# A Hyena, linear-attention and mixture-of-experts kernel: five ranked parts, rows fetched two pairs ahead, and attention's matmuls moved in the slot

## The chip, the core and the metric

The kernel runs on one core of one Trainium2 chip. The metric is the device time of one execution in microseconds. A program for one core is timed several times; a profile comes from one execution more, whose own time is given beside its span.

## What is computed

Two layers over a tensor of 2 x 2048 tokens of width 128. Each layer normalises its input, adds an attention-like branch and a mixture of experts, and keeps the residual. The second layer is where the change lies:

```
xn = _layernorm(x)
x = x + L1_attn(xn) + L1_ffn(xn)

# L1_attn: linear attention with 16 heads of 8, features elu(t) + 1
q, k = fm(x @ wq + bq), fm(x @ wk + bk);  v = x @ wv + bv
kv = einsum('bnhd,bnhe->bhde', k, v)
z = 1 / (einsum('bnhd,bhd->bnh', q, k.sum(axis=1)) + 1e-6)
out = einsum('bnhd,bhde,bnh->bnhe', q, kv, z) @ wo + bo

# L1_ffn: 8 experts, the 2 with the largest norm are used for a token
gate_hidden = einsum('nh,erh->ner', x, W_A)
scores = sqrt(sum(gate_hidden ** 2, -1));  topk_scores, topk_idx = top_k(scores, 2)
w = softmax(topk_scores)
g = einsum('ner,efr->nef', gate_hidden, W_B);  up = einsum('nh,efh->nef', x, W_up)
y = einsum('nef,ehf->neh', silu(g) * up, W_down)
out = sum over the 2 chosen experts of w * y
```

The first layer (a Hyena operator by Fourier transforms, and eight experts and a shared one computed densely) is not edited.

## The kernel before

The 4096 tokens are 32 tiles of 128 (`T`), in 8 chunks of 4 tiles (`NCH`, `TPC`). There is no scheduler: every engine has its own program, written out in one order, and semaphores join them. After the first layer's Fourier part each engine walks through a list of `SLOTS` = 90 slots.

- Slots 0 to 47 are the first layer's dense experts, six slots a chunk (`N0` = 6): TensorE does `gate0` and `up0_step`, ScalarE a silu, VectorE `product0` (L1585), GpSimd a weighting (L888), TensorE `down0_step`. Neither the gate nor the up product of the next slot goes on without the silu and the product of the one before. Between them stand the chunk's output, its normalisation, keys and values, and the second layer's router: a step "due" at offset `at` runs for chunk c in slot at + 6(c + 1).
- The router ranks tiles in parts. Before, there are 4 parts of 8 tiles (`BT`), ready with chunks 1, 3, 5 and 7. For each part VectorE runs `rank` (three steps), TensorE `counts`, VectorE `slots` (L1482 to L1495, which gives every row its place) and `weigh` (L1680 to L1683), and GpSimd `scatter` (L858) writes the tile's rows twice, once for each chosen expert, to `expert_rows` in DRAM: 64 indirect DMAs in all.
- `tables` (L1506 to L1558, four steps on VectorE) makes from the counts a list of blocks of 128 rows that all go to one expert. There are 4 lists. Blocks are worked in pairs: `NP` = 36 pairs, 71 blocks. With `LISTED` = 0, 8, 24, 40, 71 the lists begin with pairs 0, 4, 12 and 20, and may be used when all rows of 8, 16, 24 and 32 tiles have landed.
- Pair i belongs to slot i + `PAIR0`, 52 before. SyncE loads its rows (`load_rows`, L722 to L726, a ring of 5 buffers). In a slot TensorE does `turn_rows(i + 1)` (L2075), `gate_up(i)` (the L1762, L1763 and L1764 matmuls on `rows_hi`), `turn_products(i - 1)` (L2104), `down_rows(i - 2)` (L2119), and then one or two steps of attention (L2139 two steps of sums, L2145 a transpose, L2150 the output product). ScalarE does `rows_hi(i + 1)` (L1087), a copy for attention, `silu_pair(i)` (L1094), `turned(i - 1)` (L1101). VectorE does `rows_lo(i + 1)` (L1598), its attention step (L1647 to L1650, L1659), `product(i)` (L1606), `places_of(i)`, `result_rows(i - 2)` (L1628), and whatever the router still has to do for chunks 5 and 7. GpSimd sends rows and results (L873), at most 3 in a slot (`PER_SLOT`), behind the slot's `gate_up`.
- After slot 30 of the pairs the results of the first 16 tiles are read back and added; those of the last 16 after the last pair.

The waits that the text below comes back to are these, in the kernel before:

```
# SyncE, load_rows(i), where pair i opens a list
sp.wait_ge(table_in, stage_of(i) + 1)
sp.wait_ge(rows_out[stage_of(i)], 16 * 2 * BT)
# GpSimd, in a slot of the pairs
pool.wait_ge(gu_mm, min(slot - PAIR0 + 1, NP))
# TensorE, turn_rows(i)
pe.wait_ge(ld_rows[i % RING], rows_loaded(i))
```

## Time and profile before

| | |
|---|---|
| median of 3 runs | 652.54 us (646.1 to 655.0) |
| the profiled execution | 649.94 us, span 648.1 us |
| mean granted TensorE clock | 0.973 |
| TensorE busy | 567.0 us (87%) |
| VectorE busy | 447.0 us (69%) |
| ScalarE busy | 300.8 us (46%) |
| GpSimd busy | 298.2 us (46%) |

The span runs from the first to the last instruction of the program; the 1.8 us beyond it are around the program. Busy time is summed over the whole span, so it says nothing of which wait sets the pace in a stage: for that the stages have to be read apart. Matmuls overlap in the pipeline, so a busy TensorE is not one at its peak.

### The profile page before, as it was taken

To read this page: it belongs to the slowest core of one execution; us is meant where nothing else is said; L and a number is where in the kernel's file an instruction comes from. 1 tells how busy PE (TensorE), PEld (TensorE's weight loads), DVE (VectorE), ACT (ScalarE), POOL (GpSimd) and SP (SyncE) were. 2 spreads that over 40 slices of the span, in tenths; PEclk is the share of its full clock that TensorE was granted. 3 is DMA by queue.
4 is the path that set the end of the run, shared out by engine and by line. 5 is a ranking of instruction groups with operands and counts; after the bars stand their busy time and mean duration, and the time that the engine had idled before them with its cause. 6 is when DMAs were issued, how large, how long until landed. Compare 5 with 4: busy or idle time off the path is not lost.

```text
span 648.1 us, 10568 instructions
## 1 busy us (share of the span) xinstructions
PE 567.0 (87%) x3218; PEld 467.6 (72%) x3218; DVE 447.0 (69%) x1199; ACT 300.8 (46%) x558; POOL 298.2 (46%) x268
## 2 busy tenths in 40 slices
PE   5899999989899998999999999986877877888870
PEld 2879985667687677888888878765665666777660
DVE  6858998729721992344659989987787685656673
ACT  4460247655424441344577657855835433334230
POOL 5610030006561563265334458768344755666661
PEclk9999999999999998999999999997999799999995
DMA  7350031400023502133222232122211232322626
GB/s 215 128 243 17 2 129 33 97 9 2 21 110 110 172 0 65 59 93 94 75 67 79 70 100 79 39 99 68 56 55 59 59 89 71 82 73 67 208 74 223
DMA packets 48381, 54.94 MB, mean 85 GB/s; under 512 B 7029, under 2 KB 40374, under 8 KB 47271
## 3 DMA queue, kind: packets, MB, share of 16 engines
q1 hardware_dynamic: 43542, 42.99, 21.2%
q0 software_dynamic: 4320, 8.99, 4.1%
q10 hardware_dynamic: 466, 2.31, 1.6%
q8 instruction: 28, 0.46, 0.3%
q14 instruction: 25, 0.20, 0.1%
HBM read 36.22 MB, written 15.94 MB: 80 GB/s over the span
## 4 chain that ended last, share of the span: by engine, by line
PE 30%; DVE 12%; issue 9%; ACT 6%; POOL 4%; another core or an unknown queue 4%; DMA 2%; SPq 1%; POOLq 0%; ACTq 0%; DVEq 0%
PE banks L1762 4%; PE banks L1764 4%; PE banks L1763 4%; PE banks L1968 3%; PE banks L1882 2%; PE banks L2119 2%; PE banks L1874 2%; POOL arena L888 1%; PE banks L2104 1%; PE banks L1895 1%; PE banks L1896 1%; DVE arena L1606 1%; DMA arena<-result_rows 1%; PE banks L2075 1%
## 5 line engine op out<-in xcount | busy, mean ns | idle before, releaser
L873 POOL DMA_INDIRECT result_rows<-arena x71 | 69.3, 975 | 38.8 <-PE banks L1764 16.6
L858 POOL DMA_INDIRECT expert_rows<-arena x64 | 63.6, 994 | 40.6 <-issue 14.6
L822 POOL TENSOR_TENSOR arena<-arena 128x512 f32<-128x512 f32 x32 | 40.8, 1275 | 86.2 <-DVE arena L1431 86.2
L888 POOL TENSOR_TENSOR arena<-arena 128x512 f32<-128x512 f32 x32 | 42.4, 1325 | 68.2 <-DVE arena L1585 68.1
L1585 DVE TENSOR_TENSOR arena<-banks,arena 128x512 f32<-128x512 f32 x48 | 33.0, 688 | 42.5 <-PE banks L1764 33.5
L1968 PEld LDWEIGHTS banks<-arena 128*128 128x128 f32 x384 | 48.8, 191 | 6.9 <-POOL arena L888 3.0
L1968 PE MATMUL banks<-arena 128*128 128x128 f32 x384 | 51.6, 277 | 1.9 <-DVE arena L1585 1.1
L1874 PE MATMUL banks<-arena 128*128 128x512 f32 x96 | 50.5, 608 | 2.4 <-DVE arena L1431 1.1
L1882 PEld LDWEIGHTS banks<-arena 128*128 128x128 f32 x256 | 33.0, 191 | 19.0 <-POOL arena L822 14.4
L2119 PE MATMUL banks<-arena 128*128 x284 | 39.6, 284 | 7.4 <-DVE arena L1628 4.0
L1087 ACT ACTIVATE rows_hi<-banks 128x256 fp32r<-128x256 f32 (+1 forms) x36 | 13.6, 379 | 67.7 <-remote 33.6
L1149 ACT ACTIVATE arena<-banks 128x512 f32<-128x512 f32 x48 | 28.7, 599 | 35.0 <-PE banks L1764 28.6
L980 ACT ACTIVATE arena<-banks 128x512 f32<-128x512 f32 x48 | 28.7, 597 | 32.5 <-PE banks L1850 32.5
L2119 PEld LDWEIGHTS banks<-arena 128*128 128x128 f32 x284 | 35.8, 197 | 9.0 <-issue 9.0
L1429 DVE TENSOR_TENSOR arena<-banks,arena 128x512 f32<-128x512 f32 x32 | 22.1, 692 | 23.7 <-PE banks L1874 22.1
L1882 PE MATMUL banks<-arena 128*128 128x128 f32 x256 | 34.4, 277 | 4.0 <-POOL arena L822 4.0
L1762 PE MATMUL banks<-gate_up_weights_hi,rows_hi 128*128 x71 | 32.3, 454 | 6.0 <-DVE arena L1606 4.6
L1009 ACT ACTIVATE arena<-banks 128x512 f32<-128x512 f32 x32 | 19.1, 597 | 39.4 <-PE banks L1882 39.4
L1438 DVE TENSOR_TENSOR arena<-banks,arena 128x512 f32<-128x512 f32 x16 | 11.1, 692 | 36.2 <-PE banks L1896 36.2
L1762 PE MATMUL banks<-projection_hi,xnt_hi 128*128 128x384 f32 (+1 forms) x92 | 33.4, 363 | 2.6 <-DVE xnt_lo L1247 2.6
L1606 DVE TENSOR_TENSOR arena<-banks,arena 128x512 f32<-128x512 f32 (+1 forms) x36 | 24.4, 677 | 11.8 <-ACT arena L1094 10.0
L1763 PE MATMUL banks<-projection_lo,xnt_hi 128*128 128x384 f32 (+1 forms) x92 | 31.9, 347 | 0.0
(281 smaller groups left out, 1628.7 us busy)
## 6 DMA issues: line engine op xcount, KB each, us to landing
arena<-expert_weights SPq DMA_DIRECT2D x64, 128.0 KB, 3.4
arena<-expert_rows SPq DMA_DIRECT2D x71, 66.0 KB
arena<-in_x SPq DMA_DIRECT2D x8, 512.0 KB, 6.8
arena<-result_rows SPq DMA_DIRECT2D x8, 512.0 KB
arena<-in_dft_f SPq DMA_DIRECT2D x1, 2048.0 KB, 9.6
normed_hi<-xnt_hi SPq DMA_DIRECT2D x1, 2048.0 KB, 6.4
normed_lo<-xnt_lo SPq DMA_DIRECT2D x1, 2048.0 KB, 10.9
arena<-in_dft_i SPq DMA_DIRECT2D x1, 2048.0 KB, 7.7
```

Of the source, the lines that this page charges most:

```text
L822: nc.gpsimd.tensor_tensor(out=T1[:, q % 3, :], in0=T1[:, q % 3, :], in1=T2[:, q % 2, :], op=ALU.add).then_inc(y_in, 1)
L858: pool.indirect_dma_start(out=xrows, out_offset=bass.IndirectOffsetOnAxis(ap=SLOT[:, k, t:t + 1], axis=0), in_=XNF[:, t, :], in_offset=Non ...
L873: pool.indirect_dma_start(out=yrows, out_offset=bass.IndirectOffsetOnAxis(ap=DEST[:, i, n:n + 1], axis=0), in_=YB[:, i % YBUFS, n, :], in_ ...
L888: nc.gpsimd.tensor_tensor(out=AM0[slot % 2], in0=AM0[slot % 2], in1=WB0[:, m, :], op=ALU.mult).then_inc(weighted, 1)
L1585: nc.vector.tensor_tensor(out=AM0[n % 2], in0=PS[1], in1=SG0, op=ALU.mult).then_inc(mult_done, 1)
L1606: nc.vector.tensor_tensor(out=AM1[:, i % 2, 0:n], in0=pair_banks(i)[:, 0:n, F1W:2 * F1W], in1=SG1[:, i % 2, 0:n], op=ALU.mult).then_inc(mu ...
L1762: mm(o, lh, rh, start=start, stop=False, skip_group_check=True)
L1763: mm(o, lh, rl, start=False, stop=False, skip_group_check=True)
L1874: mm(PS[2 + J % 2], TURNF, ZT[:, J % 2, :], start=True, stop=True).then_inc(d_mm, 1)
L1882: ins = mm(PS[6 + q % 2][:, P * n:P * (n + 1)], T1[:, q % 3, P * n:P * (n + 1)], TURNI, start=True, stop=True)
L1968: ins = mm(PS[2][:, D * t:D * (t + 1)], AM0[n % 2][:, P * t:P * (t + 1)], DW0[:, m, :], start=False, stop=(m == N0 - 1), skip_group_check= ...
L2119: ins = mm(PS[6][:, P * s:P * (s + 1)], AMT[:, i % 2, 2 * s + f, :], DN_FLAT[:, at], start=(f == 0), stop=(f == 1), skip_group_check=True)
```

## The change

The router's 32 tiles are ranked in five parts of 8, 4, 4, 8 and 8 tiles, and the four lists are made after 12, 16, 24 and 32 tiles. `LISTED` becomes 0, 16, 24, 40, 71, so the lists begin with pairs 0, 8, 12 and 20. Of the 64 scatters 24 instead of 32 stand ahead of the pairs; from slot 51 on they come at most three a slot (in slots 51 to 53, 55 to 60 and 64 to 69), behind the slot's gate and up products. Pair 0 moves to slot 51, so every pair stands one slot earlier beside the router's steps, whose slots stay. Rows are turned two pairs ahead, with a third pair of buffers. TensorE does a slot's gate and up products first, then the rows, then attention's steps, which come one pair later. ScalarE does the silu first, VectorE the product first and the results last. From pair 13 on the down products take turns in two banks. SyncE loads the 1 MB of down weights after pair 0's rows and no longer ahead of them.

```diff
-NBT = T // BT
+NBT = 4
+RANKED = (2 * TPC, TPC, TPC, 2 * TPC, 2 * TPC)
+RANKED_AT = tuple(sum(RANKED[:n]) for n in range(len(RANKED) + 1))
+LISTED_TILES = (0, *RANKED_AT[2:])
...
-LISTED = (0, *(2 * ((2 * BT * P * (n + 1) - E1 * (P - 1)) // P // 2) for n in range(NBT - 1)), NB)
+LISTED = (0, *(2 * ((2 * P * n - E1 * (P - 1)) // P // 2) for n in LISTED_TILES[1:NBT]), NB)
...
-WEIGH_AT = (20, 18, 18, 15)
+WEIGH_AT = (20, 18, 18, 18, 15)
...
-PAIR0 = 52
+PAIR0 = 51
 SLOTS = PAIR0 + NP + 2
-SCATTER_FROM = (33, 43, 54, 64)
-ROWS_FROM = 55
 RESULT_LAG = 1
-SCATTERS = ((1, 3, 3, 1, 1, 2, 1, 1, 3), (1, 1, 1, 3, 3, 2, 2, 2, 1))
-COUNT_BANK = (3, 3, 5, 5)
-COUNT_AT = (16, 16, 17, 14)
-RANK_AT = ((13, 14, 15),) * 3 + ((12, 13, 13),)
-TABLE_AT = ((19, 20, 21, 21),) * 3 + ((16, 17, 18, 19),)
+EARLY_ROWS = dict(zip(range(33, 48), (1, 3, 3, 1, 1, 2, 1, 1, 3, 1, 1, 1, 1, 2, 2)))
+ROWS_KNOWN = {PAIR0: 16, 55: 24, 64: 32}
+DOWN_IN_TWO = 13
+COUNT_BANK = (3, 3, 3, 5, 5)
+COUNT_AT = (16, 16, 16, 17, 14)
+RANK_AT = ((13, 14, 15),) * 4 + ((12, 13, 13),)
+TABLE_AT = ((17, 18, 18, 19),) + ((19, 20, 21, 21),) * 2 + ((16, 17, 18, 19),)
...
-            sp.wait_ge(u_mm, N0 * NCH)
-            sp.dma_start(DN_FLAT, w_dn).then_inc(ld_dn, 16)
...
-                    sp.wait_ge(rows_out[stage_of(i)], 16 * 2 * BT)
+                    sp.wait_ge(rows_out[stage_of(i)], rows_sent(stage_of(i)))
...
+                if i == 0:
+                    sp.wait_ge(g_mm, N0 * NCH)
                 load_rows(i)
+                if i == 0:
+                    sp.wait_ge(u_mm, N0 * NCH)
+                    sp.dma_start(DN_FLAT, w_dn).then_inc(ld_dn, 16)
...
+                if 0 <= i < NP:
+                    product(i)
+                if 0 <= i + 2 < NP:
+                    rows_lo(i + 2)
...
                 if st < NCH:
                     gate0(slot)
-                if 0 <= i + 1 < NP:
-                    turn_rows(i + 1)
                 if 0 <= i < NP:
                     gate_up(i)
+                if 0 <= i + 2 < NP:
+                    turn_rows(i + 2)
+                for n, step in attention_steps(i - 1):
+                    attention_step(n, step)
...
                 if 2 <= i < NP + 2:
                     down_rows(i - 2)
-                for n, step in attention_steps(i):
-                    attention_step(n, step)
```

Lines of the kernel after: `turn_rows` L2098, `gate_up` L1785 to L1787, attention L2165, L2171 and L2176, `turn_products` L2128, `down_rows` L2145 on TensorE; `product0` L1606, `tables` L1527 to L1579, `weigh` L1702 to L1705 on VectorE.

TensorE before, around the transposes of pair 20's rows (slot 71, which is pair 19's):

```order
L2119 MATMUL banks<-arena 128x128
L2139 MATMUL banks<-arena 128x144 x2
L2075 MATMUL banks<-arena 128x128 x2
L1762 ISA
L1762 MATMUL banks<-gate_up_weights_hi,rows_hi 128x512
L1763 REGISTER_ALU
L1763 MATMUL banks<-gate_up_weights_lo,rows_hi 128x512
L1764 MATMUL banks<-gate_up_weights_hi,rows_lo 128x512
```

TensorE in the kernel after, around the same transposes, which now stand in slot 69, pair 18's:

```order
L1786 MATMUL banks<-gate_up_weights_lo,rows_hi 128x512
L1787 MATMUL banks<-gate_up_weights_hi,rows_lo 128x512
L2098 MATMUL banks<-arena 128x128 x2
L2176 MATMUL banks<-arena 128x128 x4
L2088 TENSOR_LOAD arena
L2088 ISA x2
L2088 TENSOR_LOAD arena
L2088 ISA x2
L2128 MATMUL banks<-arena 128x128 x4
L2145 ISA
L2145 MATMUL banks<-arena 128x128
```

The transposes of pair 20 stood ahead of pair 19's gate and up products, and now stand right behind pair 18's; attention's step moved from the end of a slot to the place behind them.

VectorE before, from `product0` of slot 34 to that of slot 36 (L1585), with sums of squares, key bias and `normed_lo` between them:

```order
L1585 TENSOR_TENSOR arena<-banks,arena 128x512
L1450 TENSOR_REDUCE arena<-arena 128x8
L1585 TENSOR_TENSOR arena<-banks,arena 128x512
L1450 TENSOR_REDUCE arena<-arena 128x8
L1568 TENSOR_TENSOR arena<-banks,arena 128x2x256
L1576 TENSOR_TENSOR normed_lo<-banks,normed_hi 128x512
L1585 TENSOR_TENSOR arena<-banks,arena 128x512
```

VectorE after, from `product0` of slot 35 (L1606) on; `product0` of slot 36 follows four rows further on:

```order
L1606 TENSOR_TENSOR arena<-banks,arena 128x512
L1469 TENSOR_REDUCE arena<-arena 128x8
L1533 TENSOR_TENSOR arena<-arena 128x8
L1527 TENSOR_SCALAR arena<-arena 128x8
L1529 TENSOR_SCALAR arena<-arena 128x8
L1530 TENSOR_SCALAR arena<-arena 128x8
L1538 COPY arena<-arena 128x8
L1543 TENSOR_TENSOR arena<-arena 128x16
L1547 TENSOR_TENSOR arena<-arena 128x16 x4
L1589 TENSOR_TENSOR arena<-banks,arena 128x2x256
L1597 TENSOR_TENSOR normed_lo<-banks,normed_hi 128x512
L1702 TENSOR_SCALAR arena<-arena 128x4
```

The first list's tables, which stood in slots 31 to 33, and the new part's `weigh` now stand between the products of slots 35 to 38.

## Rows read from the trace of the kernel before

**Rows 1.** Stretches: length, then busy us (count) of each engine, TensorE clock, DMA

```profile
core 0: us, PE busy (x) PEld busy (x) DVE busy (x) ACT busy (x) POOL busy (x), PEclk, DMA share, GB/s
447.07:510.77 63.70, 51.90 (x287) 40.80 (x285) 46.30 (x176) 37.99 (x69) 32.84 (x31) 0.93 0.20 55
510.77:562.54 51.77, 40.97 (x275) 34.57 (x274) 36.62 (x145) 17.73 (x36) 31.18 (x33) 1.00 0.28 78
562.54:623.54 61.00, 51.47 (x345) 43.27 (x343) 37.72 (x140) 20.65 (x44) 37.48 (x39) 1.00 0.35 109
```

**Rows 2.** Waits of TensorE, 447.07 to 623.54: total us, times, longest

```profile
PE banks L2145 <- DVE arena L1650: 5.1, 4, 1.7
PE banks L1762 <- DVE arena L1606: 4.6, 7, 1.2
PE banks L2104 <- issue: 4.0, 9, 1.4
PE banks L2119 <- DVE arena L1628: 4.0, 4, 1.4
PE banks L2145 <- issue: 3.5, 3, 1.7
PE banks L2139 <- issue: 2.2, 1, 2.2
```

**Rows 3.** Timeline of TensorE, from 567 us

```profile
567.17 0.66 PE L2145 MATMUL banks<-arena 128*128 128x128 f32 x4 [1.67 <-DVE arena L1650]
```

**Rows 4.** Stretches of slots 31 to 34, 35 and 36, 37

```profile
365.20:382.80 17.60, 16.97 (x104) 14.12 (x102) 16.53 (x54) 11.89 (x23) 7.94 (x7) 1.00 0.21 52
382.80:388.50 5.70, 5.55 (x37) 4.78 (x35) 4.00 (x7) 2.66 (x5) 4.61 (x6) 1.00 0.56 167
388.50:393.76 5.26, 5.26 (x35) 4.40 (x34) 5.12 (x15) 4.21 (x9) 4.75 (x5) 1.00 0.13 45
```

**Rows 5.** Stretches of VectorE: the first list's tables, summed

```profile
sum 9.07, DVE 8.27; mean DVE 2.76
```

**Rows 6.** Stretches of VectorE: slots, then weigh

```profile
459.95:462.03 2.08, 1.84 (x12) 1.00 0.14 33
462.03:462.85 0.82, 0.72 (x7) 1.00 0.24 59
```

**Rows 7.** Stretches of VectorE: the three steps of ranking 8 tiles, summed

```profile
sum 5.25, DVE 5.01; mean DVE 1.67
```

**Rows 8.** Timeline of GpSimd: the last scatters

```profile
535.51 0.96 POOL L858 DMA_INDIRECT expert_rows<-arena  x1 [1.27 <-PE banks L1764]
...
540.57 0.95 POOL L858 DMA_INDIRECT expert_rows<-arena  x1 [0.30 <-issue]
```

**Rows 9.** Timeline of TensorE: pair 17, and the rows of pair 20

```profile
539.58 0.40 PE L1764 MATMUL banks<-gate_up_weights_hi,rows_lo 128*128 x1
...
548.55 0.44 PE L2075 MATMUL banks<-arena 128*128 128x128 f32 x2 [0.47 <-DMA arena<-expert_rows]
```

**Rows 10.** Chain of waits, from the last scatter to pair 20: start, us

```profile
540.57 2.14 DMA expert_rows<-arena
...
543.27 0.84 SPq L725
...
544.85 0.69 SPq L726
...
546.78 1.55 DMA arena<-expert_rows
```

**Rows 11.** Timeline of TensorE at both clocks: pairs 11 and 12

```profile
504.49 0.79 PE L1762 MATMUL banks<-gate_up_weights_hi,rows_hi 128*128 x1 [0.95 <-DVE arena L1606]
...
506.78 0.63 PE L1764 MATMUL banks<-gate_up_weights_hi,rows_lo 128*128 x1
...
510.77 0.48 PE L1762 MATMUL banks<-gate_up_weights_hi,rows_hi 128*128 x1
```

**Rows 12.** Timeline of TensorE: the router at slot 51, and pair 0

```profile
445.35 0.80 PE L1762 MATMUL banks<-router_weights_hi,normed_hi 128*128 128x512 f32 x1 [4.31 <-ACT arena L1068]
...
447.07 0.78 PE L1762 MATMUL banks<-gate_up_weights_hi,rows_hi 128*128 x1
```

**Rows 13.** Timeline of GpSimd: scatters of slot 47

```profile
434.33 0.99 POOL L858 DMA_INDIRECT expert_rows<-arena  x1 [0.17 <-issue]
```

**Rows 14.** Timeline of SyncE: down weights, then the rows

```profile
432.12 0.34 SPq L703 DMA_DIRECT2D arena<-in_w_dn  x1
433.81 4.78 SPq L726 DMA_DIRECT2D arena<-expert_rows  x4
```

**Rows 15.** Timeline of VectorE: the last results come back

```profile
639.70 0.69 DVE L1638 TENSOR_TENSOR arena<-arena 128x512 f32<-128x512 f32 x1 [7.28 <-DMA arena<-result_rows]
```

More of the change, by code:

```diff
@@ L541, in due, with ranked_due, ranked, list_of @@
             return c - 1 if rest == 0 and 0 <= c - 1 < NCH else None
-        def odd_due(s, at):
+        def ranked_due(s, at):
             c = due(s, at)
-            return c // 2 if c is not None and c % 2 else None
+            last = [n // TPC - 1 for n in RANKED_AT[1:]]
+            return last.index(c) if c in last else None
+        def ranked(n):
+            return slice(RANKED_AT[n], RANKED_AT[n + 1])
+        def list_of(t):
+            return sum(t >= n for n in LISTED_TILES[1:])
+        def rows_sent(k):
+            return 16 * 2 * (LISTED_TILES[k + 1] - LISTED_TILES[k])
         def attention_steps(i):
@@ L599, in shares @@
         def shares():
-            rows, results, of_slot = 2 * BT * 2, 0, {}
-            for slot in range(ROWS_FROM, SLOTS):
-                known = 2 * BT * (3 if slot < SCATTER_FROM[3] else 4)
+            rows, results, of_slot = sum(EARLY_ROWS.values()), 0, {}
+            for slot in range(PAIR0, SLOTS):
+                known = 2 * max(n for at, n in ROWS_KNOWN.items() if slot >= at)
                 n = min(PER_SLOT, known - rows)
@@ L619, in results_of, with down_bank @@
             return rows
+        def down_bank(i):
+            return PS[5 if i >= DOWN_IN_TWO and i % 2 else 6]
         def pair_banks(i):
@@ L906, in _ @@
                 for bt, at in enumerate(ROOT_AT):
[L907 removed]
+                    if ranked_due(slot, at) == bt:
                         root_of_norms(bt)
[L909 to L913 removed]
+                scatter(EARLY_ROWS.get(slot, 0))
                 if slot in share:
@@ L1701, in _ @@
                     negated_mean(c)
-                c = due(slot, 6)
+                c = due(slot, 6 if slot <= N0 * NCH else 5)
                 if c is not None:
@@ L1731, in _ @@
                         norm_sum(TPC * c + t)
-                for bt in range(NBT):
+                for bt in range(len(RANKED)):
                     for part, at in enumerate(RANK_AT[bt]):
-                        if odd_due(slot, at) == bt:
+                        if ranked_due(slot, at) == bt:
                             rank(bt, part)
-                for bt in range(NBT):
-                    for part, at in enumerate(TABLE_AT[bt]):
-                        if odd_due(slot, at) == bt:
-                            tables(bt, part)
+                for k in range(NBT):
+                    for part, at in enumerate(TABLE_AT[k]):
+                        if ranked_due(slot, at) == k + 1:
+                            tables(k, part)
+                if 2 <= i < NP + 2:
+                    result_rows(i - 2)
                 if i >= BACK_AT:
```

131 lines of the change are left out of this document (63 added, 68 removed).

## The prediction, made before the changed kernel ran

> **What bounds the kernel now.** I read the page's slices first and then cut the span where the code changes its kind of work. The pairs reach from 447.07 to 623.54 us, 176.5 us for 35 pairs. In the three stretches TensorE has 51.90 + 40.97 + 51.47 = 144.3 us of work, so it stands idle for 32.1 us; every other engine is busy for less than TensorE in each of them [rows 1]. TensorE paces this part, but something holds it up in most pairs. The table of its waits tells what: it adds up to 31 us, and the six rows shown carry 23.4 of them [rows 2]. The reader should see two things there. Attention's matmuls (L2139 and L2145) wait 10.8 us, for a VectorE step that was given to the same slot; an example is the 1.67 us at 567.17 [rows 3]. And the gate and up products (L1762) wait 4.6 us for VectorE's product of the pair before. For the part ahead of the pairs I then compared TensorE with VectorE slot by slot: TensorE is busy 16.97 of 17.60 us in slots 31 to 34 and 5.55 of 5.70 in slots 35 and 36, so it sets the pace there, while VectorE has 4.00 of 5.70 us filled; in slot 37 VectorE is at 5.12 of 5.26 [rows 4].
>
> **Attention behind gate and up, rows two pairs ahead.** No instruction comes or goes; waits do. Attention's matmuls now consume what VectorE made a slot earlier, so their 5.1 + 3.5 + 2.2 = 10.8 us should go. The product now leads VectorE's slot and gate and up TensorE's, so of L1762's 4.6 us I take 4 back. L2104 waits 4.0 us on ScalarE's copy, which also comes earlier: 2.5. L2119 waits 4.0 us for a bank to be read by the result copy (L1628); that copy moves to the end of VectorE's slot, and the second bank helps from pair 13 on: 1.7 [rows 2]. Sum **-19 us**. The bounds: in the last stretch a pair takes 61.00 / 13 = 4.7 us for 4.0 of work [rows 1]; if every wait went but those of the first 12 pairs' odd ones, 26 of the 32.1 us would; if a chain through ScalarE and VectorE (silu, product, transposes, copy) keeps most periods, only attention's longest waits go, which I put at 8, the 5.1 us row and part of the 3.5 one.
>
> **Rows of pair 20.** This is the cost. The last scatters stay in slot 69 but pair 20's rows are now turned in slot 69 too, directly behind the gate and up products whose end also releases those scatters. Before, slot 69 was pair 17's and all of pair 18's slot lay between: gate and up of pair 17 ended at 539.58 + 0.40 = 539.98 and the transposes came at 548.55, after a wait of only 0.47 us [rows 9]. From the start of the last scatter (540.57) to the end of the rows' load (546.78 + 1.55 = 548.33) there are 7.76 us: 2.14 for the scatter to land, SyncE's steps, the load [rows 10]. Two of SyncE's steps are slow ones of 0.84 and 0.69; without them it would be 6.2. The scatter itself starts later than its release: GpSimd's four earlier DMAs kept it from 535.51 to 540.57 [rows 8], so after a release it comes 0.3 us later (the gap between two DMAs) to 1.5. TensorE therefore waits 0.3 + 6.2 = 6.5 to 1.5 + 7.8 = 9.3 us, and nothing can fill it, since all later work on TensorE, and `rows_hi` and `rows_lo` of pair 20 on ScalarE and VectorE, stand behind in order. I take **+7.8**, nearer to the row as measured.
>
> The Trainium skill, "DMA: Bandwidth & Descriptors", section "Anatomy of one DMA — SWDGE (gpsimd) path", gives such a DMA a fixed cost of about 2.0 us, most of it the write's receipt, so no smaller transfer would shorten it. By that rule, the trace agrees: 2.14 us [rows 10].
>
> **Clock after it.** Behind a stretch with little TensorE work before 504.49 the same 512-column matmul took 0.63 us instead of 0.40 [rows 9, 11], and pair 11 took 510.77 - 504.49 = 6.28 us, all busy, where the mean of its stretch is 51.90 / 12 = 4.33 [rows 1]. A wait of 8 us for pair 20 should do that once: **+2.0** (0 to 2.5).
>
> **Rows of pair 12.** The same, but one pair of slack: its last scatters stand in slot 60, `turn_rows(12)` in slot 61. Of 6.5 to 9.3 us one pair is covered, 4.1 us of work (40.97 / 10) or 5.3 us with its waits (63.70 / 12) [rows 1]: 2.4 to 4.0, taken **+3.1**.
>
> **Pair 0 a slot earlier.** Its rows wait for the 24th scatter, the last of which starts about 434.33 [rows 13], landed at 436.5 by the 2.14 us of [rows 10]. SyncE's loads issued at 433.81 before, behind the down weights (432.12) [rows 14]; now they issue after 437 and land near 440.5 to 441.5. Then `rows_hi`, `rows_lo` and the gate products of pair 0 come in slots where the router's matmul waits 4.31 us anyway, until 445.35, for ScalarE [rows 12]. Gate and up of pair 0 start at 446 to 447, not one slot before 447.07. I take **+1.0** for a slot's work that does not leave the path, between -3 (a slot really gained) and +5 (the loads come last, behind the 1 MB of weights moving beside them).
>
> **VectorE in slots 35 to 38.** The first list's tables, 8.27 us of work in 9.07 us [rows 5], leave slots 31 to 33 and now stand ahead of `product0` of slots 36 to 38, with the new part's `weigh`, 0.82 [rows 6]. That adds 9.9 us. Off it go 0.5 (slot 37 ranks four tiles and not eight; a step takes 5.25 / 3 = 1.75 us [rows 7], and narrower ones save little) and VectorE's idle time there, 1.70 + 0.14 = 1.84 [rows 4]: 7.5 us of overflow, since the next slot's up products need `product0`. Slots 31 to 34 give back at most 17.60 - 16.97 = 0.6 [rows 4], because TensorE was full, even though their VectorE work now is the new part's rank and `slots` (2.08 [rows 6]) instead of tables. So 6.9; between 3 (the steps share out well over four slots, TensorE one slot ahead) and 7.5 I take **+6.5**.
>
> **At nothing:** the other tables (their work stays ahead of pairs 12 and 20 by whole slots, though beside a pair one earlier), the third buffers (SBUF only), the extra bank. The end is untouched: after the last pair GpSimd's result DMAs go back to back and VectorE waits 7.28 us for them [rows 15].
>
> **The sum.** -19 + 7.8 + 2.0 + 3.1 + 1.0 + 6.5 = +1.4 on the profiled execution's 649.94: 651.3. That execution is 2.6 us below the median of three, whose runs spread over 9 us; I predict **652**. The ends of all terms give 649.9 - 26 + 6.5 + 0 + 2.4 - 3 + 3 = 633 and 649.9 - 8 + 9.3 + 2.5 + 4.0 + 5 + 7.5 = 670; they will not all fall the same way.
>
> **Rivals.** (a) **Faster: rows do not hold TensorE.** If the last scatters start promptly and SyncE's steps are short, or TensorE reaches slot 69 late because it is held elsewhere, the 7.8, 2.0 and 3.1 vanish: 651.3 - 12.9 = 638. For it: SyncE's slow steps are rare. Against: the order puts the transposes right behind the releasing product, and the one such chain that the trace shows took 7.76 us. (b) **Slower: the reorder returns only 8 us**, because the silu, product, transpose, copy chain sets a pair's time once attention's waits are gone. Price 11 us: 662. It decides if pairs 22 to 34 keep a mean period over 4.5 us, where it was 4.7; for it speaks that waits listed without a releaser ("issue") carry a third of the six rows' time [rows 2]; against it, that pairs with no attention wait run at their work. (c) **The clock falls three times**, after the waits at pair 0, 12 and 20, not once: 2 x 2.0 more, 655. Against it: from 510.77 on no stretch of the pairs shows a clock below 1.00, in spite of waits of up to 2.2 us [rows 1, 2].
>
> The Trainium skill, "TensorE: Matmul & The Clock Gate", section "HAM oscillation — how this bites in real kernels", says that a kernel which waits for DMAs between short bursts of matmuls starts each burst at the gated clock, paying each time. By that rule (c) would hold at pair 0 and 20 surely, at 12 perhaps. The trace shows it once among the pairs, before pair 11 [rows 11], and not at waits of 2 us.
>
> (d) **The change does not do what it says**: pair 0 starts no earlier. The forecast has that in it already.
>
> **Chances.** Forecast .46, (a) .22, (b) .20, (c) .07, anything else .05. The range that leaves out about 2 in 10 runs from **637 to 665**: below it lie (a) with a deep reorder gain, above it (b) with the dear ends of the DVE or start terms. About 2% is what a measurement of this kernel can tell from no change: 639.5 and 665.6. Faster than that needs (a) and a gain of 19 or more (.13), or the forecast with a reorder gain near its bound (.07): .20. Slower needs (b) and dear terms (.06) or other mishaps (.04): .10. Same: .70.
>
> **What will show it.** In the table of TensorE's waits, L2165 and L2171 (attention) should be nearly gone, and rows of L2098 on the DMA of `expert_rows` should stand near pairs 12 (2 to 4 us) and 20 (6.5 to 9.3). Behind pair 20's, a pair of about 6 us with matmuls of 0.43 us, and a clock below 1.00 in that stretch. Pairs 22 to 34 at 4.0 to 4.3 us in the mean. Slots 35 to 38 some 7 us longer, with VectorE filled. The first L1785 of pair 0 at about the old distance from slot 34, plus those 7 us. I am wrong if pair 20's wait is under 3 us, if pairs keep 4.5 us or more, or if slots 35 to 38 keep their length.

## The result, and the profile after

The changed kernel took 675.49 us (median of 4 runs, 672.25 to 677.07), the kernel before 650.37 us in the same runs: ratio 1.039, 95% interval 1.034 to 1.044. It is 25 us slower, outside the range and on the side that had a chance of one in ten. Each time in this document is the median of all runs of a kernel; the ratios leave out a run that is over 1.5% above its kernel's fastest. The profiled executions differ by 27.1 us of span (675.2 against 648.1).

Where these 27.1 us arise is read by cutting both spans at the same work. The rows give, of the kernel after, each stretch's length, then busy time (and count) of TensorE, weight loads, VectorE, ScalarE and GpSimd, then TensorE's granted clock, DMA share and GB/s: the start up to slot 31, slots 34 to 39, slot 47 to pair 0, the pairs, the end.

```profile
0.00:372.05 372.05, 351.02 (x1883) 289.09 (x1884) 245.67 (x526) 172.71 (x315) 131.78 (x108) 0.99 0.26 82
...
382.65:410.91 28.26, 22.00 (x120) 18.77 (x119) 24.57 (x72) 14.73 (x24) 17.08 (x17) 0.82 0.23 69
...
444.32:459.45 15.13, 7.67 (x27) 5.75 (x28) 8.28 (x22) 6.33 (x13) 3.22 (x3) 0.66 0.37 117
459.45:646.54 187.09, 149.07 (x901) 128.58 (x900) 122.26 (x460) 76.13 (x149) 107.59 (x108) 0.91 0.26 77
646.54:675.20 28.66, 6.93 (x44) 6.26 (x42) 13.56 (x36) 2.45 (x5) 8.13 (x9) 0.68 0.44 149
```

The kernel before, cut at the same places:

```profile
0.00:369.30 369.30, 348.46 (x1883) 287.24 (x1884) 245.60 (x526) 172.73 (x315) 131.72 (x108) 1.00 0.26 82
...
433.30:447.07 13.77, 7.13 (x34) 5.49 (x35) 11.19 (x27) 7.60 (x16) 11.11 (x11) 0.83 0.45 150
447.07:623.54 176.47, 144.33 (x900) 118.65 (x898) 120.65 (x461) 76.38 (x148) 101.50 (x102) 0.97 0.27 80
623.54:648.10 24.56, 5.52 (x37) 4.84 (x37) 11.85 (x31) 1.96 (x4) 7.28 (x8) 0.63 0.50 171
```

The unedited start is 2.75 us longer, with 2.56 us more of TensorE's busy time for the same 1883 matmuls: the clock, and no effect of the change (in a second pair of profiles below, e13 and e16, the changed kernel comes to slot 31's product 2.7 us earlier, not later). Slots 31 to 47 add 8.3, slot 47 to pair 0 1.4, the pairs 10.6, the end 4.1. In the pairs TensorE is busy 4.7 us longer for the same work at a mean clock of 0.91 (before 0.97), and idle for 38.0 us where it was idle for 32.1. The table of its waits there (total us, times, longest) says why the idle time did not fall:

```profile
PE banks L2098 <- DMA arena<-expert_rows: 14.9, 3, 8.1
PE banks L2145 <- DVE arena L1650: 7.0, 5, 2.5
PE banks L2171 <- DVE arena L1672: 4.7, 2, 2.7
PE banks L1785 <- DVE arena L1628: 4.1, 5, 1.4
```

Against [rows 2]: the three waits for rows are new, L2145 (the down products, which wait for VectorE's result copy) has grown, attention's L2171 still waits 4.7 us although its input is now asked of VectorE a slot earlier. Without the waits for rows 23.1 us of idle time are left, 8.5 less than the 31.6 of before, so other waits did shrink; how much of that is the order's, the experiments below tell. The three waits for rows in TensorE's timeline (start, us, and in brackets the idle time before it and what ended it), with GpSimd's last scatter among them:

```profile
513.84 0.69 PE L2098 MATMUL banks<-arena 128*128 128x128 f32 x2 [3.80 <-DMA arena<-expert_rows]
...
556.46 0.96 POOL L881 DMA_INDIRECT expert_rows<-arena  x1 [0.30 <-issue]
...
563.26 0.69 PE L2098 MATMUL banks<-arena 128*128 128x128 f32 x2 [8.07 <-DMA arena<-expert_rows]
...
633.71 0.69 PE L2098 MATMUL banks<-arena 128*128 128x128 f32 x2 [3.06 <-DMA arena<-expert_rows]
```

They are pairs 12, 20 and 34. The second is the sum's largest cost as it was worked out: scatter 1.27 us after `gate_up(18)` ended at 555.19, rows 6.8 us later. The third I had not seen: SyncE issues the four 512 KB loads of the first results ahead of pair 34's rows, and these are now wanted a slot earlier.

Attention's wait is the line to dwell on. All three engines around 577 us:

```profile
573.14 0.66 PE L2165 MATMUL banks<-arena 128*128 128x144 f32 x4
...
573.74 0.63 PE L2128 MATMUL banks<-arena 128*128 128x128 f32 x4
577.73 0.19 DVE L1669 TENSOR_SCALAR arena<-banks 128x32 f32<-128x32 f32 x1 [2.87 <-remote]
...
578.51 0.60 ACT L1120 ACTIVATE arena<-banks 128x512 f32<-128x512 f32 x1 [4.52 <-remote]
578.82 0.31 PEld L2171 LDWEIGHTS banks<-arena 128*128 128x128 f32 x3 [2.19 <-DVE arena L1672]
```

TensorE ended the sums (L2165) at 573.8 and the transposes (L2128) at 574.4. VectorE and ScalarE, idle and waiting for just these, began at 577.7 and 578.5. The updates of the semaphores that they waited for stand in the trace at 577.70 and 578.49: TensorE's semaphore updates reached them 3.9 and 4.1 us after the work. The example that the prediction took for a same-slot dependency, [rows 3], has the same thing behind it in the kernel before:

```profile
561.91 0.66 PE L2139 MATMUL banks<-arena 128*128 128x144 f32 x4
565.15 0.43 DVE L1598 TENSOR_TENSOR rows_lo<-banks,rows_hi 128x256 fp32r<-128x256 f32 x1 [2.85 <-ACT rows_hi L1087]
...
566.09 0.18 DVE L1647 TENSOR_SCALAR arena<-banks 128x32 f32<-128x32 f32 x1
```

The sums ended at 562.6 and their update stands at 564.66; VectorE began on them at 566.1, held at 565.15 by rows that ScalarE had got late: the update of the rows' transposes stands at 564.71, 1.9 us behind their end. Below, an update is called late when its record stands over 0.4 us behind the last end of a TensorE instruction that raises the same semaphore.

By this count none of VectorE's or ScalarE's updates in the pairs is late in any trace of the table below. It is easy to think otherwise, because a part of the update records is missing wherever TensorE's come late: the pairs have 218 of VectorE's in the first profile of the kernel before and 377 in e16, the same kernel. In the stretch below (pair 22's product, then pair 23's gate products, which wait for it) the next record of the product's semaphore stands at 570.88, yet TensorE went on 0.15 us after the product's end:

```profile
567.03 0.68 DVE L1606 TENSOR_TENSOR arena<-banks,arena 128x512 f32<-128x512 f32 x1
567.86 0.49 PE L1762 MATMUL banks<-gate_up_weights_hi,rows_hi 128*128 x1
```

Whoever takes the next record of a semaphore for that of an instruction counts such updates as late too; the "about half of the time" of the first expectation below comes of that.

### The profile page after: what moved, and what is told of

It is laid out like the page before. It is cut to its first block, busy times and chain, and to the rows that moved or that the text cites. A ratio compares the mean times of both kernels' runs of the same rounds, so it can differ in the third digit from the quotient of the medians.

```text
span 675.2 us, 10610 instructions
## 1 busy us (share of the span) xinstructions
PE 578.6 (86%) x3222; PEld 484.0 (72%) x3222; DVE 454.4 (67%) x1228; ACT 302.6 (45%) x561; POOL 298.4 (44%) x270
## 4 chain that ended last, share of the span: by engine, by line
PE 30%; DVE 14%; issue 10%; POOL 5%; ACT 3%; DMA 3%; another core or an unknown queue 2%; SPq 1%; POOLq 0%; DVEq 0%; ACTq 0%
PE banks L1785 4%; PE banks L1787 4%; PE banks L1786 4%; PE banks L1991 3%; PE banks L2145 3%; PE banks L1905 2%; POOL arena L911 2%; PE banks L1897 2%; DVE arena L1628 1%; PE banks L1918 1%; PE banks L1919 1%; PE banks L2128 1%; DVE arena L1606 1%; POOL expert_rows L881 1%
## 5 line engine op out<-in xcount | busy, mean ns | idle before, releaser
L1606 DVE TENSOR_TENSOR arena<-banks,arena 128x512 f32<-128x512 f32 x48 | 33.1, 690 | 42.2 <-PE banks L1787 33.5
L1991 PEld LDWEIGHTS banks<-arena 128*128 128x128 f32 x384 | 49.8, 194 | 5.8 <-POOL arena L911 1.7
L1113 ACT ACTIVATE arena<-banks 128x512 f32<-128x512 f32 (+1 forms) x36 | 21.3, 590 | 67.0 <-PE banks L1787 64.1
L2145 PE MATMUL banks<-arena 128*128 x284 | 42.9, 300 | 8.6 <-DVE arena L1650 7.0
L1905 PEld LDWEIGHTS banks<-arena 128*128 128x128 f32 x256 | 33.6, 194 | 19.0 <-POOL arena L845 14.4
L2145 PEld LDWEIGHTS banks<-arena 128*128 128x128 f32 x284 | 39.1, 214 | 10.2 <-issue 10.2
L1785 PE MATMUL banks<-gate_up_weights_hi,rows_hi 128*128 x71 | 32.9, 463 | 6.2 <-DVE arena L1628 4.1
L1457 DVE TENSOR_TENSOR arena<-banks,arena 128x512 f32<-128x512 f32 x16 | 11.1, 692 | 39.2 <-PE banks L1919 39.2
L1120 ACT ACTIVATE arena<-banks 128x512 f32<-128x512 f32 (+1 forms) x36 | 21.5, 596 | 35.2 <-remote 17.6
L1785 PE MATMUL banks<-projection_hi,xnt_hi 128*128 128x384 f32 (+1 forms) x92 | 33.1, 360 | 2.6 <-DVE xnt_lo L1266 2.6
## 6 DMA issues: line engine op xcount, KB each, us to landing
normed_lo<-xnt_lo SPq DMA_DIRECT2D x1, 2048.0 KB, 10.8
```

Source lines behind the costliest of these rows:

```text
L1606: nc.vector.tensor_tensor(out=AM0[n % 2], in0=PS[1], in1=SG0, op=ALU.mult).then_inc(mult_done, 1)
L1785: mm(o, lh, rh, start=start, stop=False, skip_group_check=True)
L1905: ins = mm(PS[6 + q % 2][:, P * n:P * (n + 1)], T1[:, q % 3, P * n:P * (n + 1)], TURNI, start=True, stop=True)
L1991: ins = mm(PS[2][:, D * t:D * (t + 1)], AM0[n % 2][:, P * t:P * (t + 1)], DW0[:, m, :], start=False, stop=(m == N0 - 1), skip_group_check= ...
L2145: ins = mm(down_bank(i)[:, P * s:P * (s + 1)], AMT[:, i % 2, 2 * s + f, :], DN_FLAT[:, at], start=(f == 0), stop=(f == 1), skip_group_chec ...
```

## The experiments

Eighteen runs in five groups (e1 to e4, e5 to e8, e9 to e12, e13 to e16, e17 and e18), each group on one chip; each ratio is to the kernel before, run beside it on the same chip. That kernel's median was 648.6, 653.4, 629.9, 629.6 and 652.8 us in the five. The third and the fourth group ran on the same chip, the other three on three more. Late updates of TensorE in the pairs, counted in the traces (in brackets the time that at least one stood open):

```
                               pairs, us   late updates
before, first profile            176.5      63 (53.0 us)
changed, first profile           187.1      57 (45.0 us)
order alone (e1)                 179.6      76 (56.1 us)
before, direct results (e4)      155.0      16 (14.5 us)
order, direct results (e5)       165.9      15 (12.4 us)
changed, direct results (e6)     171.7      24 (19.3 us)
before, 4th group (e16)          158.7       0
order alone, 4th (e14)           162.6       0
changed, 4th (e13)               171.5       0
before, direct, 4th (e15)        155.6       0
before, two banks, 5th (e17)     176.3      61 (52.3 us)
```

**The order alone, twice (e1 and e14).** The changed kernel with

```diff
-RANKED = (2 * TPC, TPC, TPC, 2 * TPC, 2 * TPC)
-LISTED_TILES = (0, *RANKED_AT[2:])
-PAIR0 = 51
+RANKED = (2 * TPC,) * 4
+LISTED_TILES = RANKED_AT
+PAIR0 = 52
```

and the tables of slots and banks, and the waits that go with them, of the kernel before.

> The changed slot order alone (rows two pairs ahead, third buffers, attention behind gate and up, product and silu first, down products in two banks), with the four parts, the four lists and slot 52 of the kernel before. Theory of the prediction: the waits of TensorE in the pairs were same-slot dependencies, so the order returns 19 us (8 to 26): ratio 0.96 to 0.99, and no wait of attention's matmuls stays. Rival: these waits were semaphore updates that arrive 1 to 5 us after the work has ended, in stretches where GpSimd sends indirect DMAs (such updates stand open for about half of the time in both traces); they then move to other lines, and the order returns under 8 us: ratio 0.99 to 1.01.

Measured: 652.05 us, ratio 1.006 (1.000 to 1.012). It returned nothing. Its pairs:

```profile
445.37:624.92 179.55, 144.89 (x895) 124.50 (x893) 120.57 (x457) 76.02 (x148) 102.48 (x105) 0.94 0.27 79
```

TensorE's idle time there is 34.7 us (32.1 before), 5.8 of it waits for the rows of pairs 20 and 34.

> The slot order alone once more (1.006 in the first experiment). Without late updates it should show which waits it removes and which it adds: if attention's same-slot waits are real, the ratio is now below 0.99; if they were only late updates, it is 1.00 to 1.01.

Measured in the fourth group: 636.38 us, ratio 1.011 (1.007 to 1.016), so nothing without late updates either. Its pairs, and TensorE's waits in them:

```profile
446.35:608.94 162.59, 140.18 (x895) 122.74 (x893) 120.38 (x460) 76.58 (x148) 104.03 (x105) 0.95 0.30 88
```

```profile
PE banks L2147 <- DVE arena L1652: 11.0, 7, 2.4
PE banks L2100 <- DMA arena<-expert_rows: 4.9, 2, 2.7
PE banks L1787 <- DVE arena L1630: 1.9, 2, 1.0
```

L2147 is the down product: the order brings its own waits. The idle time is 22.4 us, where the kernel before has 17.8 in the same group (e16, below). The 4.9 us of L2100, the rows of pairs 20 and 34, are as much as the difference; the other waits changed their lines and kept their sum.

**The lists alone (e2).** The changed kernel with TensorE's, ScalarE's and VectorE's rows in a slot as before, rows one pair ahead, one bank.

> The five parts, the lists of 12 to 32 tiles and slot 51 alone, with the slot order of before (rows one pair ahead, one bank for the down products). Slots 34 to 39 should be as long as in the changed kernel (28 us for 17.5) with the clock at its lower level in part of them: about +11, and pair 0 about +1.4 more. Rows of pair 20 are turned at the head of the next slot, in effect the same place, so a wait of 6 to 8 us stays and the clock falls after it: +8. If lists and order simply add up to the changed kernel's 25 us, this one is at 1.03 to 1.05 and the order alone near 1.00; if the order was worth 19 us but was eaten by its waits for rows, this one is below 1.03.

Measured: 666.23 us, 1.027 (1.021 to 1.032), a little under the range. The wait for pair 20's rows was 3.9 us, not 6 to 8: here TensorE's transposes, down products and attention of the slot stand between the releasing product and the rows. The parts about add up: 2.7% for the lists and 0.6 to 1.1% for the order, 3.9% together.

**Pair 0 back in slot 52 (e3), and scatters released a slot earlier (e8).**

```diff
-PAIR0 = 51
+PAIR0 = 52
```

> The changed kernel with pair 0 back in slot 52 and nothing else: every list has one slot more between its last scatter and the transposes of its first rows. If the waits of 8.1 us (pair 20) and 3.8 us (pair 12) come from the scatters' place, they fall to about 4 and 0, the clock stays up at pair 20, and the kernel gains 8 to 10 us on the changed one (ratio to before 1.02 to 1.03). If TensorE would wait for something else there anyway, it is within 3 us of the changed kernel.

Measured: 664.60 us, 1.021 (1.014 to 1.028). The wait at pair 20 fell from 8.07 to 4.11 us, and that at pair 12 went. The clock did not stay up at pair 20 as expected: it stood at 0.50 from 552.0 to 558.9 us.

```diff
+                    if slot > PAIR0:
+                        pool.wait_ge(gu_mm, min(slot - PAIR0, NP))
+                    scatter(share[slot][0])
                     pool.wait_ge(gu_mm, min(slot - PAIR0 + 1, NP))
-                    scatter(share[slot][0])
```

> The changed kernel, but in the pairs' slots GpSimd's scatters of rows wait for the gate and up products of the slot before, and only the result DMAs for those of the slot itself. If the waits for rows come from where the scatters are released, the 8.1 us at pair 20 fall to about 4 and the 3.8 us at pair 12 to about 0, some 8 us in all with the clock (ratio near 1.025, as with slot 52). If GpSimd's own backlog holds the scatters (five DMAs of 1.26 us stand before the last), the wait falls by 2 us at most.

Measured: 679.97 us, 1.039 (1.031 to 1.048). The wait at pair 20 fell to 4.7 us and that at pair 12 went, yet the time did not: TensorE's idle time in the pairs was 40.6 us (38.0), now on L2173, L2147 and L2130. GpSimd's earlier DMAs are the likely cause, which was not tried apart.

**Results by direct DMAs (e4, e15, e5, e6).** The results' rows then lie elsewhere, and the sums at the end add other rows.

```diff
-                    pool.indirect_dma_start(
-                        out=yrows, out_offset=bass.IndirectOffsetOnAxis(ap=DEST[:, i, n:n + 1], axis=0),
-                        in_=YB[:, i % YBUFS, n, :], in_offset=None).then_inc(st_rows[i % YBUFS], 16)
+                    at = 2 * i + n
+                    at = YFIRST + P * at if at < 2 * T else P * (at - 2 * T)
+                    pool.dma_start(yrows[at:at + P, :],
+                                   YB[:, i % YBUFS, n, :]).then_inc(st_rows[i % YBUFS], 16)
```

> The kernel before, but GpSimd sends each block of results by a direct DMA of the same bytes to consecutive rows, not by an indirect one; so the results' rows lie elsewhere and the sums at the end add other rows. If the indirect form is what delays the semaphore updates, the late ones vanish in the pairs and with them most of TensorE's 32 us of waits there: ratio 0.96 or less. If the delay comes from GpSimd's queue as such or from something else, the ratio stays 0.99 to 1.01 and late updates stay as many.

Measured: 628.50 us, 0.970 (0.965 to 0.975). Late updates fell from 63 to 16, all of them before 533 us, where the scatters of rows, still indirect, run too. Length, busy time and clock of its pairs:

```profile
450.84:605.79 154.95, 139.81 (x899) 118.00 (x898) 120.67 (x461) 77.72 (x148) 75.58 (x104) 0.98 0.31 92
```

From pair 18 on no pair of this kernel has a wait over 0.4 us before pair 35, with attention's matmuls where the kernel before has them. The direct DMAs also write to consecutive rows and not to scattered ones; which of the two matters was not tried apart.

> The kernel before with direct result DMAs once more (0.970 in the fourth experiment; other rows are added at the end). If late updates are what direct DMAs save, it saves nothing on a chip without them: ratio 0.995 to 1.005. If an indirect DMA costs by itself, it is 0.97 on any chip.

Measured: 625.31 us, 0.992 (0.988 to 0.995). Where no update is late, direct DMAs are worth 5 us and not 20.

> The slot order alone (as in the first experiment) with the results sent by direct DMAs to consecutive rows, so the output adds other rows at the end. The kernel before with direct results took 0.970 of before, and TensorE still stood idle for 15 us in its pairs. If the order removes real same-slot waits and was only masked by late semaphore updates, it now returns part of these 15: 5 to 10 us below that one, ratio 0.955 to 0.962. If the order has nothing to give even then, the ratio is 0.970 again, within 0.005.

Measured: 637.81 us, 0.972 (0.966 to 0.979). No gain on the 0.970 of the order of before.

> The changed kernel with the results sent by direct DMAs to consecutive rows (other rows are added at the end). If late updates cost the changed kernel as much as the kernel before, it gains 20 us: ratio about 1.01. Slots 34 to 39 and the waits for rows stay, so it should not come below 1.00. If it gains more than 25 us, indirect result DMAs also lengthened the waits for rows.

Measured: 653.54 us, 0.9985 (0.994 to 1.003): 0.04 less than the changed kernel, some 26 us. That is over the 25 us of the expectation, yet the waits for rows hardly moved (13.4 us in its pairs, 14.9 in the changed kernel); where the rest comes from is open. Against e4 the ratio is 1.029, over two groups.

**The change and the kernel before without late updates (e13, e16).** Both unedited.

> The changed kernel once more, unedited, beside the kernel before on one chip. In the last four runs the kernel before took 630 us and not 649 to 653, and next to no semaphore update came late, with all indirect DMAs in place. If this chip is like that one, the changed kernel shows what it costs without late updates: the order 0 to 3, the waits for rows 12, VectorE's slots 8, the clock in the rest, ratio 1.03 to 1.04. If late updates made up much of its loss, the ratio falls to 1.01 to 1.02. If this chip has late updates, the ratio is 1.034 to 1.044 again.

Measured: 654.09 us, 1.040 (1.034 to 1.045). The change costs the same with and without late updates, within the intervals.

> The kernel before, unedited, for a profile on this chip. On a chip without late updates TensorE's waits on attention's matmuls (10.8 us in the first profile) should be gone, its idle time in the pairs about 15 us, and the span near 628 us; on one with late updates it is as in the first profile.

Measured: 630.87 us, span 629.0. The pairs of e16 and, below, of e13:

```profile
446.06:604.80 158.74, 140.98 (x899) 118.13 (x898) 121.69 (x464) 78.45 (x149) 104.36 (x104) 0.98 0.31 89
```

```profile
456.50:628.02 171.52, 142.01 (x902) 123.91 (x900) 122.89 (x463) 77.32 (x150) 107.94 (x108) 0.94 0.28 84
```

TensorE's waits in them, e16 first:

```profile
PE banks L1762 <- DVE arena L1606: 4.8, 8, 1.3
PE banks L2119 <- DVE arena L1628: 2.7, 1, 2.7
PE banks L2139 <- DVE arena L1650: 2.1, 2, 1.4
PE banks L2145 <- DVE arena L1650: 1.6, 1, 1.6
```

```profile
PE banks L2098 <- DMA arena<-expert_rows: 11.4, 3, 7.4
PE banks L1785 <- DVE arena L1628: 6.7, 4, 2.7
PE banks L2145 <- DVE arena L1650: 5.9, 4, 2.5
```

Attention's 10.8 us are 3.7 here, in the same kernel. The same step of pair 22 that waited 1.67 us at 567.17 in [rows 3] starts at once:

```profile
553.73 0.66 PE L2139 MATMUL banks<-arena 128*128 128x144 f32 x4
...
556.00 0.18 DVE L1647 TENSOR_SCALAR arena<-banks 128x32 f32<-128x32 f32 x1
...
557.16 0.60 PE L2145 MATMUL banks<-arena 128*128 128x128 f32 x4
```

**Filler for the clock (e7, e11).** Ahead of the transposes of three pairs, and in the second kernel ahead of the router's matmul in slot 51:

```diff
-                pe.wait_ge(ld_rows[i % RING], rows_loaded(i))
...
+                for _ in range({0: 7, 12: 3, 20: 9}.get(i, 0)):
+                    split_product(PS[0], (GUH_FLAT[:, 0:P], GUL_FLAT[:, 0:P]), (GUH_FLAT[:, 0:4 * P], GUL_FLAT[:, 0:4 * P]))
+                pe.wait_ge(ld_rows[i % RING], rows_loaded(i))
```

> The changed kernel with filler matmuls (128 x 512, their products are overwritten) ahead of the transposes of pairs 0, 12 and 20: 21, 9 and 27 of them, a little less than the waits there at the 0.23 us that one takes at the upper clock. The waits for rows themselves stay. If the lower clock after these waits is a cost of its own, the work behind them runs at 2.4 GHz (granted clock 1.00 around pairs 0, 12 and 20) and the kernel gains 3 to 6 us on the changed one (ratio 1.03); if idle time was what counted and the clock beside it nothing, the kernel is within 2 us of the changed one or slower.

Measured: 670.49 us, 1.023 (1.015 to 1.032), where the changed kernel has 1.039. The two were not run on the same chip. The ratios put the gain at 10 us, the two profiled spans at 3.7, and the ends of the intervals at 1 to 19: there is a gain, and its size is not settled. The clock did not stay up: it no longer fell ahead of pair 0, but stood at 0.50 for 3.4 us each from 513.4 and 554.4 us (6.8 and 10.3 us in the changed kernel). The pair with the wait for pair 20's rows took 12.19 us in place of 14.32, at a clock of 0.91:

```profile
555.66:567.85 12.19, 11.37 (x58) 9.32 (x57) 2.77 (x9) 1.58 (x3) 2.87 (x3) 0.91 0.18 51
```

> The kernel before with 15 filler matmuls (128 x 512, 3.5 us at 0.23 each, their products are overwritten) ahead of the router's matmul in slot 51, where TensorE waits 4.3 us for ScalarE and the clock falls for 7 us. If the clock is a cost of its own there, pair 0 starts at the upper clock and 1 to 3 us are won (ratio 0.995 to 0.998); if TensorE's filler delays something, or the pairs are held by other engines, no gain.

Measured: 631.77 us, 1.002 (0.998 to 1.006). This one decides nothing: on this chip the kernel before has no fall of the clock at pair 0 in the first place (e16, 1.00 there), so there was nothing to win back.

**Mends (e9, e10, e12).** On the order alone: the result copy ahead of the router's steps; then pair 34's rows ahead of the first results too; then both on the changed kernel, with slot 52.

```diff
                 if 0 <= i < NP:
                     places_of(i)
+                if 2 <= i < NP + 2:
+                    result_rows(i - 2)
...
-RESULTS_BEFORE = 34
+RESULTS_BEFORE = 35
```

> The slot order alone (first experiment, 1.006 of before) with one part of it undone: VectorE's result copy stands again behind the places, ahead of the router's steps, not at the end of its slot. TensorE's down products wait 10 us on that copy in the order-alone kernel, most of it in pairs 0 to 17. If the late copy is what the order pays, these waits fall under 4 us and the ratio to 0.99 to 1.00. If it was waited for because semaphore updates come late, they stay and so does 1.006.

Measured: 634.23 us, 1.005 (1.001 to 1.008), where e14 has 1.011 (1.007 to 1.016) on the same chip; the intervals overlap. The wait on the copy went from the list, and L1787's on the product took its place:

```profile
PE banks L1787 <- DVE arena L1630: 9.5, 9, 1.8
PE banks L2100 <- DMA arena<-expert_rows: 5.4, 2, 2.8
```

> As the kernel before it in this list, and SyncE issues the loads of pair 34's rows ahead of the first results' loads, not behind them. TensorE waited 1.6 us in the order-alone kernel and 3.1 in the changed one for pair 34's rows, which rows two pairs ahead want a slot earlier. That wait should go: 1 to 2 us, ratio 0.99 to 1.00. If the results' sum at the end is late for it instead, nothing is won.

Measured: 633.71 us, 1.004 (1.000 to 1.009); of the two waits for rows one is left, 2.7 us, and nothing was won that can be told from e9.

> The changed kernel with three mends: pair 0 in slot 52, the result copy ahead of the router's steps, pair 34's rows loaded ahead of the first results. Slot 52 alone gave 1.021. If the three costs add up, this one is 6 to 8 us lower, 1.008 to 1.012, and what is left over the kernel before is VectorE's extra work in slots 35 to 38 (about 8 us). If it is at 1.00 or below, that work was no cost of its own.

Measured: 643.47 us, 1.018 (1.012 to 1.024), hardly below the 1.021 of slot 52 alone. The waits on the copy and for pair 34's rows are gone, and those for the product stand at 11.3 us (L1785). The two mends on top of slot 52 won nothing that can be told from noise.

**Two parts alone on the kernel before (e17, e18).** Two banks for the down products from pair 13 on; and, on top, silu and product directly behind the next pair's rows.

```diff
+                if 0 <= i < NP:
+                    product(i)
...
                 if 0 <= i < NP:
-                    product(i)
                     places_of(i)
```

> The kernel before with one part of the change: from pair 13 on the down products take turns in two banks. On the chip without late updates TensorE waited 4.5 us on L2119 for the bank, 3.5 of them behind pair 13. They should go, with about 1 us of clock behind pair 17: 3 to 4 us, ratio 0.994 to 0.997. If another wait takes their place (the copy of the transposed products, VectorE's product), the ratio is 1.00.

Measured: 652.61 us, 1.001 (0.998 to 1.004), in a group with late updates. The bank's line waits 1.9 us (5.1 in the first profile), and attention's transposes 11.1 (8.6).

> As the kernel before it in this list, and ScalarE's silu and VectorE's product stand directly behind the next pair's rows (still one pair ahead), not behind the router's and attention's steps. TensorE's gate and up products waited 4.6 to 4.8 us for that product in the kernel before. If they waited for its place in VectorE's row, 2 to 4 us more are won: ratio 0.988 to 0.994. If the router's steps that are now pushed back are waited for in their turn, nothing is won.

Measured: 663.85 us, 1.017 (1.011 to 1.022), with 38.5 us of idle time in the pairs (30.6 in the kernel with two banks alone). TensorE's waits named the product's place (5.0 us on L1767 in e17), and moving it forward, with the silu, cost 11 us. These two moves are part of the order.

## Why the prediction was wrong

**The step that failed is the first term, "no instruction comes or goes; waits do", -19 us.** Measured: +0.6% and +1.1%, some +4 and +7 us. So the sum missed by 23 to 26 us there, which is its whole error: the other terms, +20.4 together, are met in their sum (not one by one) by the 25 us measured less the order's 4 to 7, and by the 17 us of the lists alone. Of those 4 to 7 us some 5 are waits for the rows of pairs 20 and 34; the waits that the term was about shrank by 3 us in e1 and by 0.3 in e14, in place of 19. Three things stood behind it.

First, the waits were not the dependencies I took them for. The table said that L2145 waited for VectorE's L1650, which was true for 5.1 of the 10.8 us (the other 5.7 stand there as "issue", without a releaser, and I put them down to VectorE too); why L1650 was late I did not ask. In the example it was late because TensorE's own updates had come late. Without late updates the same kernel shows 3.7 us on attention's lines and not 10.8, and its pairs take 158.7 us and not 176.5: 14 of the 32 idle us were no property of the order at all. That alone does not explain the miss, for the order returns nothing on either chip. A later place for the matmul cannot win back a delay that then meets another line: in the changed kernel it stood on L2171 and L2145.

Second, where the updates are prompt there was something to win (17.76 us of idle time in e16), and the order still lost. TensorE's down products wait for the result copy, which I had counted as a gain of 1.7. In e13, in slot 54, VectorE goes through the places, the router's `slots` and `weigh` for 8 tiles, a sum of squares and attention's step before it comes to the copy, and TensorE's down products of the next slot wait for it:

```profile
476.76 0.16 DVE L1503 TENSOR_TENSOR arena<-banks,arena 128x8 f32<-128x8 f32 x1
...
479.50 0.17 DVE L1705 TENSOR_TENSOR arena<-arena 128x8 f32<-128x8 f32 x1
479.59 0.68 DVE L1469 TENSOR_REDUCE arena<-arena 128x8 f32<-128x512 f32 x1
480.18 0.42 DVE L1650 TENSOR_TENSOR arena<-banks,arena 128x256 f32<-128x256 f32 x1
```

```profile
480.86 1.15 PE L2145 MATMUL banks<-arena 128*128 x8 [2.50 <-DVE arena L1650]
```

I moved the copy "to the end of VectorE's slot" and did not list what stood ahead of it there. When it is moved back (e9) the product is waited for instead. And silu and product first, which I had booked as 4 us won, cost 11 us when they were tried without the rest (e18). Which chain of steps holds a pair once the copy is mended was not isolated; that stays open.

Third, pair 34: rows two pairs ahead must pass the results' loads on SyncE's queue. The prediction looked only at queues that the change edits. The wait is 3.06 us in the first profile and 1.6 in e1; taking it away (e10) changed the time by nothing that can be told from noise.

**Rows of pair 20: right.** Predicted 6.5 to 9.3 us, taken 7.8; measured 8.07 and, in e13, 7.36, behind the last scatter as worked out. Slot 52 halves it, as it should. Rival (a), rows that do not hold TensorE, is out with it.

**Rows of pair 12: right.** 2.4 to 4.0, taken 3.1; measured 3.80 and 3.08.

**Clock: too small in the first profile.** I took 2.0 us for one fall. TensorE was busy 4.7 us longer in the pairs for the same work (in e13 against e16 only 1.0 us), and the granted clock fell to 0.50 six times in them (near 473, 514, 534, 558, 609 and 633 us) and not once. The rival with falls at pairs 0, 12 and 20 was right on its places (the one at pair 0 came ahead of it, from 448.7 to 459.0), and its 6.0 us stand against 4.7 in the pairs and 2.9 more between the products of slots 31 and 38: a shorter wait did it too (1.62 us in pair 2, with the clock at 0.50 from 473 us). The Trainium skill, "TensorE: Matmul & The Clock Gate", section "HAM oscillation — how this bites in real kernels", says that such falls are paid each time; by that rule, the trace agrees here. What e7 adds is a rough size of what filler gives back: 4 to 10 us of the 25 by its middle values, 1 to 19 by its intervals.

**Pair 0 in slot 51: right in the first profile, by luck.** Taken +1.0, measured +1.4; against e16 it is +4.9 (15.1 us from slot 47's product to pair 0 in e13, 10.2 in e16), the upper bound that was given. TensorE waits 5.62 us for pair 0's rows in the changed kernel (5.68 in e13); the kernel before stood still in that stretch of its first profile as well (4.31 us, for ScalarE), so the two differ little there. As rival (d) has it, pair 0 starts no earlier: at 459.45 and not at 447.07.

**VectorE in slots 35 to 38: right in kind, over its bound in size.** Taken +6.5 of 3 to 7.5. From slot 31's product to slot 38's it was 8.4 us more (36.40 against 27.99), 5.5 of it idle time of TensorE and 2.9 clock; VectorE's busy time rose from 25.06 to 32.17. e13 against e16 gives 8.3. The bound left the clock out.

**The end:** taken at nothing, measured +4.1, 2.8 of it a wait of attention's last transposes, which now come after pair 35's slot began: the update of the sums that ended at 645.46 stands at 649.13, 3.7 us late. In e13 the end is +0.8.

**The rivals.** (b), the reorder returns less, was the right one of the four, with the wrong floor: I let it return 8, and it returned less than nothing. Its chain from the product on is what TensorE waits for in e9, once the copy is mended (9.5 us on the product). Its point of decision, the mean period of pairs 22 to 34, I set at 4.5 us; it was 64.92 / 13 = 5.0. In e13 it is (628.02 - 573.01) / 13 = 4.2, and the kernel is as slow: with waits that sit elsewhere, that mean decided nothing.

## What to carry to other kernels

When an engine waits for another's step, follow the chain one more step back before you move anything: a consumer that starts microseconds after the producer's end, while it is idle, waits for neither; its cause is an update on its way. And a missing record of an update is no late one: see whether the waiting engine went on. Of a step that is moved to the end of a slot, list what now stands ahead of it in the fullest slots, and who waits for it; of data asked for earlier, list all that its queue issues in between. A wait for rows that is counted from the last scatter to the landing can be sized well from one chain in a trace; add the clock behind it.

## What the hardware showed that was not expected

In the first profiles and in three groups of runs semaphore updates of TensorE came up to 6.5 us late; with all indirect DMAs in place, at least one stood open for a quarter to a third of the time in the pairs. In the two groups where the kernel before took 630 us and not 650 none did, with the same kernels. Those two groups ran on one and the same chip, the other three on three others; the chip of the first profiles is not on record. Direct DMAs for the results removed three quarters of the late updates and 20 us where there were such, and 5 us where there were none. So the indirect DMAs of the results, or the scattered rows that they write, bring most of them about in some groups and not in others. What sets these apart (the chip, or something beside the kernel on it) stays open: the record fits the chip, and no run here could choose it.

The same code thus runs 3% apart, while the ratio of the changed kernel to the kernel before stayed at 1.039 and 1.040: that ratio carries over here, single times don't. It need not hold for every change: direct result DMAs are 0.970 in one group and 0.992 in another.
